# Selective scan on one core: a fourth of 16 states weighted on VectorE

## The reference, cut to what matters

```python
def _selective_scan(x, W_x, W_z, W_params, conv_w, W_dt, b_dt, A_log, D_param, W_out):
    ...
    dt = softplus(dt_unproj @ W_dt.T + b_dt)
    u = silu(conv(x @ W_x.T))
    A = -exp(A_log)
    A_tilde = exp(dt[..., None] * A)
    B_tilde = where(abs(A) < 1e-08, dt[..., None], (A_tilde - 1.0) / (A + 1e-10))
    def step(h, ins):
        A_t, B_t, Bp_t, Cp_t, u_t = ins
        h = A_t * h + B_t * Bp_t[:, None, :] * u_t[:, :, None]
        y_t = einsum('bn,bdn->bd', Cp_t, h)
        return (h, y_t)
    ...
    y = y + u * D_param
    y = y * silu(z)
    return y @ W_out.T
```

## Time and profile before

| | us |
|---|---|
| median of 3 runs (2067.32 to 2070.0) | 2068.37 |
| profiled execution, its own time | 2066.44 |
| its span, first to last instruction | 2064.7 |
| scan, from its first POOL instruction to the second feed-forward | 1272.0 to 1830.2 |
| DVE products of line 1994 in the scan | 26 |
| POOL products of line 1664 in the scan | 102 |

### The profile page before, as it was taken

How to read it: one execution, slowest core, us unless ns; L and a number is a source line. 1 busy time by engine, 2 the same in 40 slices (tenths; PEclk the granted TensorE clock), 3 DMA queues, 4 the chain that set the end, 5 groups by cost and what they waited for, 6 DMA issues and landing times. The chain is left out here.

```text
span 2064.7 us, 25864 instructions
## 1 busy us (share of the span) xinstructions
PE 1896.0 (92%) x7474; PEld 838.6 (41%) x7474; DVE 1651.7 (80%) x2569; ACT 1078.7 (52%) x1479; POOL 716.5 (35%) x479
## 2 busy tenths in 40 slices
PE   7998999999999999997999997888898888689998
PEld 3441232332332332321666663333333333256665
DVE  4889898898998998983565565999999999955554
ACT  3441666666666666665233434765676667333221
POOL 3653100000000000003000004999999999810000
PEclk9996899999999999998999998999999999999999
DMA  3562122121321224202501002455544545400000
GB/s 100 131 140 62 37 48 43 42 50 42 63 46 43 42 48 127 42 17 67 133 21 41 21 11 97 130 134 137 133 129 138 135 121 165 109 1 21 21 21 21
DMA packets 104235, 151.20 MB, mean 73 GB/s; under 512 B 14961, under 2 KB 58241, under 8 KB 102561
## 3 DMA queue, kind: packets, MB, share of 16 engines
q1 hardware_dynamic: 104096, 149.48, 28.4%
HBM read 118.75 MB, written 30.29 MB: 72 GB/s over the span
## 5 line engine op out<-in xcount | busy, mean ns | idle before, releaser
L922 DVE TENSOR_REDUCE mx<-max_bank 128x1 f32<-128x512 f32 x960 | 618.2, 687 | 63.3 <-PE max_bank L831 62.9
L908 ACT ACTIVATE probs<-score_bank 128x1024 f32<-128x1024 f32 x512 | 496.8, 1021 | 298.8 <-PE score_bank L845 298.6
L831 PE MATMUL max_bank<-ks,qs 96*128 96x512 bf16 x960 | 335.4, 390 | 0.0
L845 PE MATMUL score_bank<-qs,ks 99*128 99x512 bf16 x1024 | 313.2, 389 | 15.3 <-issue 10.7
L1721 PE MATMUL ys_bank<-outs,rec_diag 128*128 128x512 f32 x512 | 256.4, 634 | 68.4 <-POOL outs L1664 45.4
L1656 POOL TENSOR_TENSOR ring<-u,bc 128x1024 f32<-128x1024 f32 x128 | 303.1, 2383 | 0.6 <-DMA bc<-bc_scr 0.5
L891 PE MATMUL o_bank<-probs,vg 128*32 128x512 f32 x2048 | 275.3, 610 | 9.9 <-DVE o_sb L941 9.2
L1862 ACT ACTIVATE a_bank<-dt,decay_s 128x512 f32<-128x512 f32 x256 | 170.6, 686 | 147.9 <-DVE ring L1986 95.1
L1664 POOL TENSOR_TENSOR outs<-ring,bc 128x1024 f32<-128x1024 f32 x102 | 242.4, 2376 | 14.8 <-DVE ring L1986 14.8
L1334 PE MATMUL y_bank_f<-wpr_f,hid_f 128*128 128x256 f32 x1024 | 236.4, 379 | 0.0
L786 POOL CAST neg_parts<-neg_max 16x128 bf16<-16x128 f32 x31 | 8.8, 284 | 655.8 <-DVE neg_max L935 655.8
(11 more groups left out here) (233 smaller groups left out, 2009.0 us busy)
## 6 DMA issues: line engine op xcount, KB each, us to landing
bc<-bc_scr SPq DMA_DIRECT2D x128, 512.0 KB, 4.9
qk_parts<-parts SPq DMA_DIRECT2D x128, 96.0 KB, 1.9
qs<-qk_parts SPq DMA_DIRECT2D x128, 64.0 KB, 4.3
o_scr<-o_sb SPq DMA_DIRECT2D x32, 256.0 KB, 2.1
ks<-qk_parts SPq DMA_DIRECT2D x16, 384.0 KB, 4.6
xn_s<-xn_scr SPq DMA_DIRECT2D x8, 515.0 KB, 6.4
xin<-in_x_dram SPq DMA_DIRECT2D x8, 512.0 KB, 4.1
ks<-qk_parts SPq DMA_DIRECT2D x16, 256.0 KB, 3.5
```

The source lines that it names most:

```text
L831: nc.tensor.matmul(max_bank[(r + a) % MB][:], qs[r][0:SROWS, half, j, qt * P:(qt + 1) * P], ks[r][0:SROWS, j, kh * TW:(kh + 1) * TW], star ...
L845: mm = nc.tensor.matmul(score_bank[pair][:, j % 2], ks[r][0:MROWS, j, kt * P:(kt + 1) * P], qs[r][0:MROWS, qh, j, :], start=True, stop=True)
L908: nc.scalar.activation(probs[:, s % 2, 2 * pair:2 * pair + 2], score_bank[pair][:], ACT.Exp, scale=SOFTMAX_SCALE).then_inc(probs_ready, 1)
L922: nc.vector.tensor_reduce(mx[:, a // HU, a % HU:a % HU + 1], max_bank[(r + a) % MB][:], AX_X, ALU.max)\
```

## The change

State 15 joins the states that DVE weights, in the seven tiles that aren't the last: the tuple `ON_DVE` gets a fourth entry. All that depends on it (where the recurrence writes, which engine makes the product, which semaphore and count the others wait for, whether ACT's copy stands ahead of the decay) follows from `on_dve` and `weighted_by`. For state 15 the product stands on DVE in the first unit of the next tile. The last tile's tuple has 15 already and stays.

```diff
@@ -1557,7 +1557,7 @@
     AHEAD = 3
     LAG = 3
     D_UNIT = 8
-    ON_DVE, ON_DVE_LAST = (3, 7, 11), (3, 6, 9, 12, 15)
+    ON_DVE, ON_DVE_LAST = (3, 7, 11, 15), (3, 6, 9, 12, 15)
     with ExitStack() as ctx:
```

## The result

| | before | after |
|---|---|---|
| median, us (20 runs each) | 2068.57 | 2071.27 |
| lowest to highest, us | 2064.24 to 2072.77 | 2067.87 to 2080.6 |
| span of the profiled execution, us | 2064.7 | 2069.0 |
| its scan, first scale on DVE to first matmul of the last feed-forward, us | 554.43 (1275.73 to 1830.16) | 559.93 (1274.58 to 1834.51) |

The ratio is 1.0021, with a 95% interval of 1.0012 to 1.003. The kernel became slower, as forecast, but by less than the 7.9 us that I gave it: 2.7 us between the medians, 4.3 by the ratio. In the profiled pair the scan grew by 5.5 us; its span grew by 4.3, because the scan began 1.15 earlier in that execution.

A forecast was written before the change was run, and what follows sets the result against it. VectorE was taken to bound the scan, with GpSimd only just fast enough. Seven added products at 1.13 us gave +7.9 us, from 2068.37 to 2076.3 us; GpSimd's relief counted as nothing. The range was 2073.8 to 2080.0 us.

The forecast's parts named there:

- The bound: In the scan, VectorE sets the pace at 67.88 us a tile; GpSimd follows with 1.2 us to spare.
- What is removed from POOL, at nothing: GpSimd's queue loses 16.1 us over seven tiles, counted at nothing; PE's earlier product of state 15 also gives nothing.
- What is added, 1.13 a product: One more VectorE product in each of seven tiles costs its pitch, 1.13 us, upper end 1.32.
- The hand-over on ACT: At the tile boundary, ScalarE copies the state 1.30 after the product's start, begins the decay at 1.59; it just fits.
- The large wait swallows nothing: VectorE's largest wait, 1.84 us in tile 2, is anchored at state 7's product, moves along and absorbs nothing.
- The smaller ones could go; 0.9 us in all is the bound: Small VectorE waits, 0.36 in tile 2, the same in tile 4, 0.2 on POOL, could absorb at most 0.9 us.
- what delays the scan delays the end by the same: From the second feed-forward's start at 1830.16 the last-ending chain is PE's alone, so scan delay passes to the end.
- POOL as the bound: Rival: GpSimd sets the scan's pace, so its relief gives -4.3 us, 2064.1; chance 0.05.
- The product swallowed by waits on ACT: Rival: VectorE's waits on ScalarE after state 7 absorb about 7.6 of 7.9 us, 2068.7; chance 0.05.
- The stall: Rival: late decay at tile boundaries makes +14.2 to +20.5 us, 2082.6 to 2088.9; chance 0.10 with milder forms from +9.2.

The follow-up runs named there:

- Relief alone: The kernel before, with GpSimd's product of state 15 cut to one column in seven tiles, VectorE as before: scan 554.25 us, ratio 1.0001.
- cost alone: The changed kernel with an unused GpSimd product of the same size put back after state 15's scan in seven tiles: scan 560.02 us, ratio 1.0036.
- product twice: The changed kernel with VectorE's product of state 15 made a second time, into its own buffer, in seven tiles: scan 567.82 us, ratio 1.0063.
- the repeated one: Both kernels profiled a second time, unedited: scan 554.76 us before, 560.02 us after, ratio 1.0028.
- the change backwards: The kernel before with VectorE weighting states 3 and 11 alone in seven tiles, so GpSimd has 30 products a tile: scan 567.88 us.
- the tiny write: The kernel before with a one-column write added on VectorE, at the place of state 15's product, in tiles 1 to 7: scan 554.81 us.
- the product cut: The changed kernel with VectorE's product of state 15 cut to one column in seven tiles: scan 552.59 us.
- other states: Kernel before, other VectorE states, seven tiles: 3, 9 and 13, scan 552.01 us; 5, 9 and 13, 552.00; 2, 6 and 10, 561.68; 1, 5 and 9, 551.00.

## Why the prediction was wrong, point by point

**The bound: right.** DVE sets the pace. Relief alone 554.25 against 554.43 and 554.76, cost alone equal to the change. Occupancy (POOL 67.21, DVE 64.97 of 67.80) would have named the wrong engine.

**What is removed from POOL, at nothing: right for POOL, not for PE.** POOL's load is worth nothing, by the same two runs, and its rest in tiles 0 to 6 became 21.5 us, not 28. But the same paragraph says that PE gets the product of state 15 earlier and "this gives nothing". With the relief alone it gave 0.6 to 1.4 us up to the last product, the gaps below.

**What is added, 1.13 a product: right.** 1.13 in the trace after, 1.11 in the run with two products, 1.06 against one cut to a column.

**The hand-over on ACT: right** to the hundredth (copy at 1.30, decay at 1.59), and no stall came.

**The large wait swallows nothing: right.** 1.84 in tile 2 before, 1.84 and 1.85 in all even tiles but the first after, and in the run with the product twice.

**"The smaller ones could go; 0.9 us in all is the bound": this step failed.** The bound was drawn from waits that the list names, before the last tile. The runs show three terms, 2.5 us in all in the profiled pair and 2.7 in the repeated one:

- Hiccups at fixed places of the streams, 0.36 on DVE and 0.27 on ACT, that any shift of the code can remove. I had seen the first as "0.5 us for itself" and left it in place; the second is no wait of its own in DVE's list, as it only makes a wait for ACT longer (1.48 in place of 1.21).
- Gaps between states 3 and 7 in tiles 2 to 5, 1.4 us in the profiled execution and 0.56, in tile 6, in the repeated one; none in the changed kernel. Half of this was listed, and counted (0.36 in tiles 2 and 4); the rest were gaps below 0.2. In tile 2 the origin can be followed: DVE waited for ACT's decay, ACT for PE's step size, and PE's taps ahead of it took longer. PE before, then after:

```profile
1424.30 5.40 PE L1695 MATMUL work<-xn_s,wtap_s 128*128 128x512 f32 x8 [2.05 <-DVE x L1958]
```

```profile
1425.43 4.72 PE L1695 MATMUL work<-xn_s,wtap_s 128*128 128x512 f32 x8 [0.25 <-DVE x L1958]
```

  The same eight matmuls took 5.40 us at a granted clock of 0.68 and 4.72 at 0.78 (3.70 in the repeat after). The wait itself isn't the cause: in the repeat before it was 2.05 too, and they took 3.70 at 1.00, with no gap. In tile 6 the repeat before has the gap and the relief alone hasn't:

```profile
1697.30 5.49 PE L1695 MATMUL work<-xn_s,wtap_s 128*128 128x512 f32 x8 [1.04 <-DVE x L1958]
```

```profile
1693.55 3.70 PE L1696 MATMUL work<-xn_s,wtap_s 128*128 128x512 f32 x8 [0.58 <-DVE x L1959]
```

  It is the same in every tile of the nine profiles that come ahead of the change backwards, before and after included. These matmuls take 5.40 us or more in just the seven tiles that have a gap (four before, one in the repeat, two with the tiny write), and 4.9 or less elsewhere. Those three profiles are the ones in which POOL makes the whole product of state 15; there PE rests 2.7 to 3.9 us ahead of the gate in tiles 2 to 6. In the other six it has that product earlier and rests 4.4 to 7.4 us. Then the level falls before or with the sum that stands ahead of the taps, and comes back sooner. That the longer rest is what moves the fall fits all of these rows; no run changes it alone.
- The end of the scan, 0.43 us in the first pair and 1.61 in the repeated one. I didn't examine it, taking the last product's delay for the end's ("what delays the scan delays the end by the same"). It is 9.91 us from the start of the last product to the feed-forward before and 11.10 in the repeat, but 9.48 in the changed kernel and 9.49 and 9.48 with the product twice and the cost alone. Here are three windows, 17 to 5 us ahead of the feed-forward, in the order before, before again, after (length, PE busy, then the granted clock):

```profile
1813.20:1825.20 12.00, 10.55 (x20) 0.86 0.00 1
```

```profile
1815.50:1827.50 12.00, 10.79 (x20) 0.80 0.00 1
```

```profile
1817.50:1829.50 12.00, 9.19 (x20) 1.00 0.00 0
```

The same 20 matmuls, at a granted clock of 0.86, 0.80 and 1.00. PE in time order there, in the repeated kernel before, then in the one after:

```profile
1814.56 3.78 PE L1680 MATMUL work<-xn_s,wz_s 128*128 128x512 f32 x4 [1.93 <-ACT sz L1820]
1818.13 8.16 PE L1721 MATMUL ys_bank<-outs,rec_diag 128*128 128x512 f32 x16
```

```profile
1818.18 1.98 PE L1680 MATMUL work<-xn_s,wz_s 128*128 128x512 f32 x4 [1.39 <-ACT sz L1820]
1820.00 3.60 PE L1721 MATMUL ys_bank<-outs,rec_diag 128*128 128x512 f32 x8
1824.52 3.78 PE L1721 MATMUL ys_bank<-outs,rec_diag 128*128 128x512 f32 x8 [0.92 <-POOL outs L1664]
```

Four matmuls take 3.78 us at the level of 1.2 GHz and 1.98 at that of 2.4 GHz. Before, the slow level lasts into this stretch, PE has no rest in the last 16 matmuls and the sum of the scan ends on it. After, PE has even to wait 0.92 for POOL, and the end hangs on the last products. All four profiles of kernels with the full new product (after twice, cost alone, product twice) have the fast level here; the five with the old states or the product cut (before twice, relief, tiny write, product cut) have 0.79 to 0.86, and so have the five with other states. What in the change decides over the level isn't settled: PE had waited in both, as the brackets show.

**The time.** About 7.95 put in, less 0.63, 1.4 and 0.43, is 5.5. In the repeated pair it is 0.63, about 0.5 and 1.61, which leaves 5.3. A difference of 5.5 is 1.0027 of the kernel, within the intervals of both measurements (1.0012 to 1.003, 1.0017 to 1.004). The medians of the first, 2.7 us apart, are less than that; what the stages before the scan did in those runs isn't shown here. The forecast stood on a full price of 7.9 with the scatter of three runs around it, where 20 runs of before alone spread from -4.3 to +4.2, so the scatter in the range was drawn from too few runs. The median of before moved by only 0.2 from 3 runs to 20, so this isn't what missed.

**The rivals.** POOL as the bound: refuted here, true with one product more on it. The product swallowed by waits on ACT: not as proposed, though the idea holds if the product is put where the wait is. The stall: didn't come. One reading of the page was off, without effect on the sum: POOL is near nine tenths in slices 26 to 35, not to 36.

## What to carry to other kernels

When two engines are both near full, look at who waits for whom before moving work: here 0.2 against 3.8 us named the bound, and occupancy named the other. The full price of an instruction added to the bound engine is its pitch, but take it only down to the stage's last hand-over, and examine that one separately: which engine ends it, and how fast it ran in that execution. Compare marks along the stage too, not only its length: with POOL's relief alone a gain of 0.6 to 1.4 us and a longer end cancelled each other. A wait on the bound engine is the place to put added work, and whether it is really fillable depends on what the waited-for engine was itself released by.

## What the runs showed of the hardware

Two pauses of 0.36 and 0.27 us sat at fixed places of unrolled code and came back in each of the three profiles of that code. The one on VectorE vanished with a single tiny instruction more on it, and both vanished with the change. And TensorE's clock level, though TensorE isn't the bound of the scan, reached its end: the tails differ by 1.2 us between two executions of one kernel, and by 0.4 to 1.6 between the two kernels, with the same matmuls. It reached the middle too: eight matmuls that took 5.40 us or more, in place of 3.6 to 4.9, came with a gap of 0.24 to 0.66 us on VectorE.
